# First stage of an attention block in fp32 on one Trainium2 core: rotary products taken from PSUM, sums on GpSimd, transposes of unsplit head pairs, stores of two tiles

## The reference

```python
# h = layernorm(x) * (1 + scale) + shift, rows of 128
q = (x @ Wq).reshape(b, l, H, HD).transpose(0, 2, 1, 3)
k = (x @ Wk).reshape(b, l, KV, HD).transpose(0, 2, 1, 3)
v = (x @ Wv).reshape(b, l, KV, HD).transpose(0, 2, 1, 3)
...
q = q * cos + _rotate_half(q) * sin
k = k * cos + _rotate_half(k) * sin
attn = jnp.einsum('bhqd,bhkd->bhqk', q, k) / math.sqrt(HD)
```

## Time and profile before

| | |
|---|---|
| median of 3 runs | 1317.8 us (1313.16 to 1318.82) |
| profiled execution | 1316.46 us, its span 1314.7 us |
| busy over the span | PE 85%, DVE 80%, POOL 65%, ACT 56% |
| mean granted PE clock | 0.943 of full |
| first stage | 0 to 163.2 us, mean granted PE clock 0.87 from 60 to 112 us |

### The profile page before, as it was taken

One profiled execution on the slowest core, in us unless ns is written; L12 is line 12 of the kernel. 1 busy time (PEld: TensorE's weight loads), 2 busy tenths in 40 slices (PEclk: granted clock), 3 DMA queues, 4 the chain that ended last, 5 costly groups with the idle time before them and its releaser, 6 DMA issues. The chain is left out here.

```text
span 1314.7 us, 23737 instructions
## 1 busy us (share of the span) xinstructions
PE 1115.1 (85%) x8256; PEld 692.6 (53%) x8256; DVE 1049.2 (80%) x2026; ACT 735.6 (56%) x1512; POOL 849.0 (65%) x488
## 2 busy tenths in 40 slices
PE   5776579999999999999999999467777896778788
PEld 3554535544455454555445548234555684455578
DVE  6898577777777777777777746599999589999957
ACT  3666625555555555555555551257676755777664
POOL 4556216566566666656656664698789249999916
PEclk9888769999999999999999999789898997999899
DMA  7567932142413314241331001000111100111111
GB/s 230 136 173 198 283 80 57 42 97 65 105 42 86 76 42 97 65 105 38 83 83 52 23 17 56 34 17 19 27 28 28 31 3 8 27 28 29 30 31 33
DMA packets 95237, 88.91 MB, mean 68 GB/s; under 512 B 22884, under 2 KB 74768, under 8 KB 95120
## 3 DMA queue, kind: packets, MB, share of 16 engines
q1 hardware_dynamic: 95120, 87.41, 26.2%
HBM read 53.57 MB, written 24.25 MB: 59 GB/s over the span
## 5 line engine op out<-in xcount | busy, mean ns | idle before, releaser
L738 ACT ACTIVATE E<-psum,keybias_sb 128x1024 f32<-128x1024 f32 x256 | 274.8, 1112 | 249.1 <-PE psum L862 235.9
L765 DVE CUSTOM_DVE_ANT_0 junk<-psum,alibi 128x1024 bf16<-128x1024 f32 x256 | 309.4, 1209 | 93.0 <-PE psum L836 80.2
L684 POOL TENSOR_TENSOR xpos_sb<-xpos_sb,E 128x1024 f32<-128x1024 f32 x96 | 231.2, 2408 | 130.7 <-ACT E L738 126.2
L872 PE MATMUL psum<-E,V 128*64 128x512 f32 x1024 | 248.0, 605 | 0.0
L836 PE MATMUL psum<-KH,QH 64*128 64x512 f32 x512 | 124.7, 481 | 20.9 <-DVE M L765 16.7
L688 POOL TENSOR_TENSOR xpos_sb<-xpos_sb 128x1024 f32<-128x1024 f32 x32 | 76.1, 2377 | 90.7 <-DVE xpos_sb L775 90.7
L1195 ACT ACTIVATE E_att<-S_att,nmax_att 128x128 f32<-128x128 f32 x256 | 99.0, 389 | 43.7 <-DVE nmax_att L1229 43.6
L1142 POOL TENSOR_TENSOR rinv_att<-ss_up_att,minus_half 128x16 f32<-128x16 f32 x32 | 120.8, 3775 | 2.7
L872 PEld LDWEIGHTS psum<-E,V 128*64 128x64 f32 x1024 | 62.1, 136 | 112.7 <-issue 105.7
L836 PEld LDWEIGHTS psum<-KH,QH 64*128 64x128 f32 x512 | 50.6, 191 | 124.1 <-DVE M L765 92.6
L782 DVE RECIPROCAL XF<-XF 128x128 f32<-128x128 f32 x64 | 60.4, 948 | 64.1 <-ACT XF L715 64.1
(11 more groups left out here) (145 smaller groups left out, 2399.9 us busy)
## 6 DMA issues: line engine op xcount, KB each, us to landing
qa_scratch<-tT SPq DMA_DIRECT2D x32, 512.0 KB, 4.1
QH<-qa_scratch SPq DMA_DIRECT2D x64, 256.0 KB, 4.2
QL<-qa_scratch SPq DMA_DIRECT2D x64, 128.0 KB, 4.2
XF<-inverse_scratch SPq DMA_DIRECT2D x64, 128.0 KB, 2.9
vp_att<-v_att SPq DMA_DIRECT2D x64, 128.0 KB, 2.3
k_scratch<-tT SPq DMA_DIRECT2D x16, 256.0 KB, 4.6
KH<-k_scratch SPq DMA_DIRECT2D x16, 256.0 KB, 3.9
KL<-k_scratch SPq DMA_DIRECT2D x16, 256.0 KB, 5.1
```

The lines of the kernel that those rows point to most:

```text
L684: pool.tensor_tensor(sum_p[:, s, :], first, E[:, k % 4, :], ALU.add)\
L738: act.activation(E[:, k % 4, :], scores(k % 2), ACT.Exp, bias=kb).then_inc(exp_done, 1)
L765: dve.tensor_tensor_reduce(junk[:, :], banks(max_bank(i, k), 2), alibi[:, s, :], -1.0, BIG, ALU.add, ALU.min, M[:, s, k:k + 1]).then_inc(m ...
L872: last = pe.matmul(banks(6 + i % 2)[HD * ch:HD * ch + HD, :], V[:, g, k, :], E[:, k % 4, ch * 512:(ch + 1) * 512], start=(k == 0), stop=(k ...
```

## The change

The first stage is rewritten. DVE multiplies the projected queries and keys by cosine and by sine directly from PSUM, in three parts of 8, 8 and 4 heads (`products`), so `take_raw` and its buffer go. POOL adds (`rotated`). PE transposes pairs of unsplit heads, 10 of 128x128 for a tile (`transposed`), which leaves the even head of a pair in partitions 0 to 63 and the odd one in 64 to 127. ACT writes the high parts out of PSUM (`high_parts`, into `tH`), and DVE the low parts (`low_parts`, into `tL`). SP stores two tiles at once (`store_pair`): eight DMAs, each from 64 partitions, with 1 KB for each partition and head. The normalisation moves to ACT (`ln_apply`), its statistics are taken ahead, and 1/sqrt comes in three batches. V's scratch is laid out by token, so its store has 1 KB pieces and its load 256 B pieces.

```diff
-    v_d = nc.dram_tensor("v_scratch", (B, KV, P, TB, HD), F32, kind="Internal").ap()
+    v_d = nc.dram_tensor("v_scratch", (B, P, TB, KW), F32, kind="Internal").ap()
...
-    sp.dma_start(V[:, s, :, :], v_d[g // KV, g % KV]).then_inc(ld_kv[s], 16)
+    sp.dma_start(V[:, s, :, :], v_d[g // KV, :, :, g % KV * HD:(g % KV + 1) * HD]).then_inc(ld_kv[s], 16)
...
-    tT = sb("tT", [P, 2, H + KV, P], F32R)
+    tH = sb("tH", [P, 2, NBLK, 2 * P], F32R)
+    tL = sb("tL", [P, 2, NBLK, 2 * P], F32R)
...
+    def need_v_sent(eng, t):

         if t >= 2:
-            eng.wait_ge(sems[(t - 2) // TB][t % 2], count * ((t - 2) % TB // 2 + 1))
+            eng.wait_ge(v_out[(t - 2) // TB][t % 2], 16 * ((t - 2) % TB // 2 + 1))
+    def need_pair_sent(eng, t):
+        pair = t // 2 - 2
+        if pair >= 0:
+            eng.wait_ge(t_out[pair // (TB // 2)][pair % 2], 128 * (pair % (TB // 2) // 2 + 1))
...
+    PARTS = ((0, 8), (8, H), (H, H + KV))
+    NPT = len(PARTS)
+    LN_BATCHES = ((0, 2), (2, TB), (TB, T))
+    def part(tensor, s, n, t):
+        a, b = PARTS[n]
+        return tensor[:, s, a // 2:b // 2, t % 2 * P:t % 2 * P + P]
+    def turned_part(n):
+        a, b = PARTS[n]
+        return banks(4 + n)[:, 0:(b - a) // 2 * P].rearrange("p (j c) -> p j c", c=P)
...
-                sp.dma_start(v_d[t // TB, :, :, t % TB, :].rearrange("g p d -> p g d"),
-                             v_sb[:, s, :].rearrange("p (g d) -> p g d", d=HD)).then_inc(v_out[t // TB][s], 16)
+                sp.dma_start(v_d[t // TB, :, t % TB, :], v_sb[:, s, :]).then_inc(v_out[t // TB][s], 16)
...
-                if t == TB + 2:
+                if t == TB + 1:
...
+            def store_pair(t, s):
+                if t % 2 == 0:
+                    return
+                b, pair = t // TB, t // 2
+                tiles = slice(t % TB - 1, t % TB + 1)
+                for done, tensor, row in ((high_done, tH, 0), (low_done, tL, HD)):
+                    for d, first, heads in ((qa_d, 0, H), (k_d, H, KV)):
+                        need(sp, done, NPT * t + (NPT if first else NPT - 1))
+                        for a in range(2):
+                            sp.dma_start(d[b, a::2, row:row + HD, tiles, :].rearrange("j p t c -> p j (t c)"),
+                                         tensor[HD * a:HD * a + HD, pair % 2, first // 2:(first + heads) // 2, :]
+                                         .bitcast(F32)).then_inc(t_out[b][pair % 2], 16)
+            over_tiles([(first_heads, 3), (store_pair, 3), (store_v, 2)])
...
+            def ln_rstd(n):
+                a, b = LN_BATCHES[n]
+                pool.wait_ge(ln_step, 2 * b)
+                pool.tensor_scalar(var_eps[:, a:b], mv[:, a:b, 1], EPS, None, ALU.add).then_inc(eps_done, 1)
+                pool.wait_ge(eps_done, n + 1)
+                pool.tensor_tensor(rstd[:, a:b], var_eps[:, a:b], minus_half[:, 0:b - a], ALU.pow)\
+                    .then_inc(rstd_done, 1)
+            def second_batch(t, s):
+                if t == TB // 2:
+                    ln_rstd(2)
+            def rotated(t, s):
+                need(pool, cos_done, NPT * (t + 1))
+                need(pool, sin_done, NPT * (t + 1))
+                need(pool, tr_done, NPT * (t - 1))
+                m = HD // 2
+                pool.tensor_tensor(qk[:, s, :, 0:m], t1[:, s, :, 0:m], t2[:, s, :, m:HD], ALU.add)\
+                    .then_inc(sum_done, 1)
+                pool.tensor_tensor(qk[:, s, :, m:HD], t1[:, s, :, m:HD], t2[:, s, :, 0:m], ALU.add)\
+                    .then_inc(sum_done, 1)

             pool.memset(minus_half[:, :], -0.5).then_inc(half_set, 1)
             pool.wait_ge(half_set, 1)
-            over_tiles([(ln_rstd, 0), (sin_part, 2)])
+            for n in range(2):
+                ln_rstd(n)
+            over_tiles([(second_batch, 1), (rotated, 2)])
...
+            def ln_apply(t, s):
+                if t in (a for a, _ in LN_BATCHES):
+                    act.wait_ge(shift_done, 1 + [a for a, _ in LN_BATCHES].index(t))
+                need(act, xT_done, t - 1)
+                act.activation(xn[:, s, :], X[:, t, :], ACT.Identity, bias=shift[:, t:t + 1],
+                               scale=rstd[:, t:t + 1]).then_inc(xn_done, 1)
             def take_v(t, s):
-                need(act, qkv_done, t + 1)
-                need_sent(act, v_out, 16, t)
+                need(act, v_mm, t + 1)
+                need_v_sent(act, t)
...
+                if t % 2 == 0:
+                    need_pair_sent(act, t)
+                for n in range(NPT):
+                    need(act, tr_done, NPT * t + n + 1)
+                    act.activation(part(tH, t // 2 % 2, n, t), turned_part(n), ACT.Copy,
+                                   scale=HD ** -0.5 if n < NPT - 1 else 1.0).then_inc(high_done, 1)
+            over_tiles([(modulate, 1), (ln_apply, 0), (take_v, 2), (high_parts, 3)])
...
+            def stats_ahead(t, s):
+                if t == 0:
+                    dve.wait_ge(ld_x[1], 16)
+                if t < TB // 2:
+                    for n in range(2):
+                        ln_stats(TB + 2 * t + n)
+                elif t == TB // 2 + 1:
+                    ln_shift(2)
...
+            def products(t, s):
                 dve.wait_ge(ld_rope, 16)
+                need(dve, sum_done, 2 * (t - 1))
+                for n, (a, b) in enumerate(PARTS):
+                    need(dve, qk_mm, NPT * t + n + 1)
+                    for out_, row, done in ((t1, 0, cos_done), (t2, 1, sin_done)):
+                        table = rope[:, t % TB, row, :][:, None, :].to_broadcast([P, b - a, HD])
+                        dve.tensor_tensor(out_[:, s, a:b, :], ps_qk[:, a:b, :], table, ALU.mult).then_inc(done, 1)
             def low_parts(t, s):
+                if t % 2 == 0:
+                    need_pair_sent(dve, t)
+                for n in range(NPT):
+                    need(dve, high_done, NPT * t + n + 1)
+                    dve.scalar_tensor_tensor(part(tL, t // 2 % 2, n, t), turned_part(n),
+                                             HD ** -0.5 if n < NPT - 1 else 1.0,
+                                             part(tH, t // 2 % 2, n, t).bitcast(F32), ALU.mult, ALU.subtract)\
+                        .then_inc(low_done, 1)
+            dve.wait_ge(ld_x[0], 16)
+            for t in range(2):
+                ln_stats(t)
+            ln_shift(0)
+            for t in range(2, TB):
+                ln_stats(t)
+            ln_shift(1)
+            over_tiles([(products, 2), (first_rows, 2), (low_parts, 3), (stats_ahead, 1)])
...
+                for n in range(2):
+                    need(pe, sin_done, NPT * (t - 1) + n + 1)
+                    need(pe, cos_done, NPT * (t - 1) + n + 1)
+                    pe.matmul(banks(n), hT[:, s, :], w_sb[:, n * 512:(n + 1) * 512], start=True, stop=True)\
+                        .then_inc(qk_mm, 1)
+                need(pe, sin_done, NPT * t)
+                need(pe, cos_done, NPT * t)
+                pe.matmul(banks(2)[:, 0:KW], hT[:, s, :], w_sb[:, QW:QW + KW], start=True, stop=True)\
+                    .then_inc(qk_mm, 1)
                 need(pe, v_copied, t)
+                pe.matmul(ps_v, hT[:, s, :], w_sb[:, QW + KW:], start=True, stop=True).then_inc(v_mm, 1)
+            def transposed(t, s):
+                if t == 0:
+                    pe.wait_ge(mod_step, 2 + 3 * B)
+                need(pe, sum_done, 2 * (t + 1))
+                for n, (a, b) in enumerate(PARTS):
+                    need(pe, low_done, NPT * (t - 1) + n + 1)
+                    for j in range((b - a) // 2):
+                        src = qk[:, s, a + 2 * j:a + 2 * j + 2, :].rearrange("p h d -> p (h d)")
+                        last = pe.transpose(turned_part(n)[:, j, :], src, ident[:, :])
                     last.then_inc(tr_done, 1)
+            over_tiles([(x_transposed, 1), (project, 2), (gate_rows, 2), (transposed, 3)])
```

More of the change, by code:

```diff
@@ L343, in take_v @@
                     def take_v(t, s):
-                        need(act, qkv_done, t + 1)
-                        need_sent(act, v_out, 16, t)
+                        need(act, v_mm, t + 1)
+                        need_v_sent(act, t)
                         act.activation(v_sb[:, s, :], ps_v, ACT.Copy).then_inc(v_copied, 1)
-                    def take_raw(t, s):
-                        need(act, qkv_done, t + 1)
-                        need(act, cos_done, t - 1)
-                        need(act, sin_done, t - 1)
-                        act.activation(raw[:, s], ps_qk, ACT.Copy).then_inc(raw_done, 1)
@@ L369, in _ @@
-                    over_tiles([(high_parts, 4), (take_raw, 2), (take_v, 2), (modulate, 1), (take_transposed, 5)])
+                    def high_parts(t, s):
+                        if t % 2 == 0:
[4 more added lines that the diff above has]
+                                           scale=HD ** -0.5 if n < NPT - 1 else 1.0).then_inc(high_done, 1)
@@ L463, in _, with gate_rows @@
```

(23 more changed lines are left out.)

105 lines of the change are left out of this document (20 added, 85 removed).

## The result

The changed kernel takes 1319.68 us (median of 20 runs, 1316.85 to 1324.89) against 1317.21 us for the kernel before, timed beside it (20 runs, 1313.16 to 1321.33): a ratio of 1.0021, with a 95% interval of 1.0011 to 1.0031. It is slower by 2.5 us, a little more than its runs are uncertain and less than the 0.5% by which the chances were given. The forecast was 1310.5 us. The profiled execution took 1320.01 us, with a span of 1318.2 us.

A forecast was written before the change was run, and what follows sets the result against it. Once the engines were freed, stores at 215 GB/s in a 15.5 us ring were to bind the first stage, ending it at about 156 us against 163.2; -7.2 us applied to the median gave 1310.5 us, range 1281 to 1324.

The forecast's parts named there:

- the engines: First stage, per tile: DVE 4.6 us, POOL additions 2.96, ACT 2.8, PE 4.7, with DVE and POOL not excluding each other.
- the forecast tile of 4.7 us: First stage: a tile would cost 4.7 us if nothing but the engines held it, ending the stage near 105 us.
- the ring: First stage: `take_v` waits for V's store queued behind a pair, whose completion needs `take_v`: 15.5 us for two tiles.
- the rate of a single pair: First stage's stores from 64 partitions: 215 GB/s, so 12.2 us for a pair's 2.62 MB.
- the end of the last computation: End of the first stage: the last high and low parts take 11 us after tile 14 passes at 140.0, ending at 151.
- 17.1 + 12.2: First stage's store queue: 3.67 MB of `first_heads` loads (17.1 us at 215 GB/s) ahead of pair (8, 9) (12.2 us).
- so the last issue is at about 156: End of the first stage: SP's last store issue at about 156 us against 163.2 today, a gain of 7.2 us.
- some 150 pieces for each engine: Depth of the DMA queue in the first stage, about one pair, read from a K store's issue of 5.77 us.
- which nothing waits for: V's loads after the first stage: 256 B pieces take half a microsecond more each for eight, with nothing waiting.
- without that cover: V's loads in 256 B pieces would cost 4 us if something did wait for them.
- Slower: Rival, 13%: first-stage stores at the SBUF copies' rate or below; at 194 GB/s 1321 us, at 185 1326.
- The first rival: Rival, 25%: 64-partition halves don't bind first-stage stores; at 289 or 334 GB/s the kernel takes 1290 or 1281 us.

The follow-up runs named there:

- e_best: Changed kernel with stores across 128 partitions, V's store ahead of the pair, and V's layout of the kernel before: 1274.54 us, 0.9659 of the kernel before.
- e_wide: Changed kernel with scratch laid out so each store of a pair spans all 128 partitions, four stores instead of eight: 1291.74 us, 0.9802 of the kernel before.
- e_vfirst: Changed kernel with V's store issued ahead of the pair of tiles instead of behind it: 1306.66 us, 0.9922 of the kernel before.
- e_tailv: Changed kernel with the last pair's low-part stores issued from ScalarE's queue and V's layout of the kernel before: 1318.63 us, 0.9983 of the kernel before.
- e_vlayout: Changed kernel with V's scratch, store and load as in the kernel before (2 KB load pieces): 1317.56 us, 0.9999 of the kernel before.
- e_vlate: Changed kernel with V's load of a new group issued behind the inverse row's store and spread in the attention stage: 1313.69 us, 0.9947 of the kernel before.
- e_final: e_best with V's load of a new group issued behind the inverse row's round trip, as in e_vlate: 1269.56 us, 0.9619 of the kernel before.

## Why the prediction was wrong

**Right: the engines.** VectorE's three low parts took 1.62 us and the six products 3.14, for 1.55 and 3.05 forecast, GpSimd's additions 1.53 each for 1.48, and neither made the other wait. e_best shows the forecast tile of 4.7 us running.

**Right: the ring, and the rate of a single pair.** The first pair was issued at 34.05 (33 forecast); single pairs went at 206 to 210 GB/s (215); the period was 15.6 us (15.5). `take_v` passed at 48.4, 64.0, 79.6, 95.9, 121.7 and 137.3, where 47.0, 62.5, 78.0, 93.5, 124.5 and 140.0 were forecast. ScalarE's waits there came to 71.7 us (some 60 forecast), though each was 8.4 to 11.0 us (20.5 across the loads) and not 6 to 8; the DMA share from 47 to 150 us was 0.80 at 200 GB/s, not 0.9 or more. e_wide and e_vfirst each cut the ring at one of its two links and got back 28.9 and 13.5 us of the stage.

**Right by luck: the end of the last computation.** It was at about 150, for 151 forecast. But the ring was 2.4 us late at tile 10 (95.9) and 2.8 early at tile 12 (121.7): the loads and the pair behind them took 25.8 us, not 31.0. The term "17.1 + 12.2" put 215 GB/s on a pair that stood in a full queue, and it moved at up to 377. Two errors cancelled there.

**Wrong: "so the last issue is at about 156".** It began at 160 and ended at 162.09. I had read the depth of the queue from one slow K store, "some 150 pieces for each engine", and so let SyncE put in nearly a whole pair ahead of its transfer. The trace shows the issue held much earlier: in a pair, with nothing ahead of it, the first two Q stores go in within 1.3 us, and the K stores behind them take 4.4, about 2.2 each, close to the 2.5 us that a Q store needs at 208 GB/s. SyncE spent 11.0 us on issuing the last pair, whose bytes need 12.2 at my rate, so it is free only when nearly all is out. My reason for a late issue wasn't there either: the pair before was issued from 138.7, 2.8 us earlier than I had it, and fully in at 149.9, before the last one could start (151.1). The stage ends with its last issue, not with the last computation, so those 6 to 7 us were lost there, and e_tailv got 2.7 of them back by giving the last stores a second queue. In all the kernels of the table the next stage begins 0.4 to 1.1 us behind the last issue. What fills up stays open. It isn't a number of pieces alone: in e_wide a store of 1024 pieces and one of 256 go in within 1.0 us, where here two of 512 hold up one of 128. And it isn't the bytes queued: behind the loads, in a full queue, the four stores of high parts went in within 2.6 us (106.26 to 108.90). I took the length of one wait for the depth of a queue.

**Wrong: V's 256 B pieces, "which nothing waits for".** VectorE waits for them, one step removed: they stand in SyncE's queue ahead of the inverse row's round trip. The bound that I gave "without that cover", 4 us, was about the size (3.3 profiled, 2.9 by the ratios of the changed kernel and e_vlayout), but the cover wasn't there, and the time isn't lost where the bound put it, in the landing of V: with the load behind the round trip, e_vlate, the same pieces cost next to nothing (the attention stage is 0.7 us longer than in e_final, where V has 2 KB pieces). I had looked for who reads V, and not for what is queued behind it.

Together: 7.1 us less gained in the stage and 3.3 lost after it are nearly the whole of the difference between the -7.2 us forecast and the +3.5 of the profiled spans (+2.5 by the medians). Of the rivals, none was this. "Slower" was put on the transfer rate, which for single pairs was near 215. The first rival, at 1281 to 1290 us, is what e_wide made true by design, at 1291.7 with V's loss still in it.

Some of the prediction's sums don't follow from its own numbers. The copies of the earlier trace rows give 187 GB/s over 14 bins, not 194; the stage end moves by 0.48 us for each GB/s around 215 (102.5 us of transfers over 215), not 0.75; and the chances, added up by its rivals, give about 0.30 to the same and 0.10 to slower, not 0.27 and 0.13. None of these decided the outcome.

## What to carry to other kernels

Before crediting a faster engine, find what a stage's end waits for: here it was the issue of the last store, and the issue of many stores in a row can last about as long as their transfer (11.0 of 12.2 us). When a small transfer that someone waits for shares a queue with large ones, its place matters more than its size: moving V's store ahead of a pair gave 13.5 us of the stage in one line, and moving V's load behind a round trip made the attention stage 5.8 us shorter than in the changed kernel, and 3.4 in e_final than in e_best. And a layout of buffers that splits a store into halves of 64 partitions should be costed as such from the start, at a rate that depends on how much is queued (208 GB/s for a single pair, up to 377 in a full queue).

## What was not expected of the hardware

A delay of about 0.5 us at head 8 came with a loss of 2.2 us there (2.63 in the changed kernel, 0.43 in e_vlayout), because TensorE's granted clock then fell, from 1.00 to a mean of 0.67 over 5 us; six kernels show such falls at different groups, eight show none, and idle times of up to 2.52 us passed without one. V's load costs the round trip even in 2 KB pieces: in e_best 2.3 to 3.6 us at the group heads with it ahead, in e_final 1.6 to 2.4 with it behind. Stores from 64 partitions, 206 to 210 GB/s for a single pair, reached 377 in a full queue. And a DMA issue on a second queue isn't free of the first one's: SyncE's two Q stores went from 1.29 us to 4.66 when ScalarE's stood beside them.
